# A hybrid attention block on one core: stacks of keys and queries in two buffers by halves, feed-forward buffers of their own, and distances spread over 120 quarters

## The reference

```python
dist = _pairwise_l2(x @ w3d.T + b3d)              # sqrt of the sum of three squares
scores = -dist[:, None, :, :] * scale             # causal, then softmax, then @ V, @ wo
...
r = jax.nn.sigmoid(jnp.einsum('btc,dc->btd', xr, W_r))
k_act = jnp.square(jax.nn.relu(jnp.einsum('btc,dc->btd', xk, W_k)))
out = r * jnp.einsum('btc,dc->btd', k_act, W_v)
...
x = x + attn_a(layernorm(x)); x = x + ffn(layernorm(x))
x = x + attn_b(layernorm(x)); x = x + ffn(layernorm(x))
```

## Time and profile before

| | us |
|---|---|
| median of 3 runs | 2093.7 |
| lowest, highest | 2085.45, 2105.44 |
| the profiled execution's own time | 2109.85 |
| its span | 2108.1 |
| busy in it: PE, DVE, ACT, POOL | 1849.2, 1467.0, 1323.7, 728.2 |

### The profile page before, as it was taken

One profiled execution on the slowest core, in us unless ns is written; L12 is line 12 of the kernel. 1 busy time (PEld: TensorE's weight loads), 2 busy tenths in 40 slices (PEclk: granted clock), 3 DMA queues, 4 the chain that ended last, 5 costly groups with the idle time before them and its releaser, 6 DMA issues. The chain is left out here.

```text
span 2108.1 us, 32379 instructions
## 1 busy us (share of the span) xinstructions
PE 1849.2 (88%) x9842; PEld 922.5 (44%) x9842; DVE 1467.0 (70%) x4288; ACT 1323.7 (63%) x2585; POOL 728.2 (35%) x879
## 2 busy tenths in 40 slices
PE   5677898889997999889998899979998899988986
PEld 4453443335543455434543355434544345322423
DVE  5576778767676677667786667766776677768642
ACT  3564355876569565776758665695657766455664
POOL 1342332234333253333443243333532334312313
PEclk8797899999998999999999899989999999989998
DMA  3006113111131112410132111311124101322000
GB/s 85 1 23 123 26 56 67 31 31 32 55 76 31 31 31 82 80 21 12 41 110 42 31 31 56 76 31 31 34 83 76 22 11 41 99 33 50 13 21 20
DMA packets 64346, 97.26 MB, mean 46 GB/s; under 512 B 15655, under 2 KB 58029, under 8 KB 58030
## 3 DMA queue, kind: packets, MB, share of 16 engines
q1 hardware_dynamic: 64174, 95.20, 20.2%
HBM read 61.09 MB, written 33.55 MB: 45 GB/s over the span
## 5 line engine op out<-in xcount | busy, mean ns | idle before, releaser
L973 ACT ACTIVATE pt<-exp_bank 128x512 f32<-128x512 f32 (+1 forms) x1216 | 698.9, 582 | 526.6 <-PE exp_bank L935 521.0
L989 DVE CUSTOM_DVE_ANT_0 max_bank<-max_bank,mask 128x128 f32<-128x128 f32 (+3 forms) x1024 | 501.8, 500 | 400.9 <-PE max_bank L922 386.4
L922 PE MATMUL max_bank<-ks,qs 96*128 96x512 bf16 (+3 forms) x1536 | 523.5, 346 | 85.9 <-DVE piece_max L992 44.9
L935 PE MATMUL exp_bank<-qs,ks 98*128 98x512 bf16 (+3 forms) x1536 | 515.4, 342 | 40.0 <-ACT pt L973 37.0
L992 DVE TENSOR_REDUCE piece_max<-max_bank 128x1 f32<-128x512 f32 x512 | 344.1, 686 | 94.4 <-PE max_bank L922 90.2
L954 PE MATMUL o_bank<-pt,v 128*17 128x512 f32 (+3 forms) x3072 | 334.1, 508 | 13.7 <-POOL pt L1011 11.0
L922 PEld LDWEIGHTS max_bank<-ks,qs 96*128 96x128 bf16 x1536 | 150.9, 99 | 399.5 <-DVE piece_max L989 140.9
L1011 POOL TENSOR_SCALAR_AFFINE_SELECT pt<-pt 128x512 f32<-128x512 f32 x256 | 171.5, 670 | 412.6 <-ACT pt L973 411.8
L935 PEld LDWEIGHTS exp_bank<-qs,ks 98*128 98x128 bf16 x1536 | 152.4, 100 | 236.0 <-ACT pt L973 118.5
L633 PE MATMUL side<-vp,p 128*128 128x260 f32 x576 | 171.4, 423 | 28.7 <-ACT p L560 21.0
L412 ACT ACTIVATE xh<-xs,shift,rstd 128x256 f32<-128x256 f32 x256 | 149.7, 596 | 47.8 <-POOL shift L401 47.8
(11 more groups left out here) (119 smaller groups left out, 2348.4 us busy)
## 6 DMA issues: line engine op xcount, KB each, us to landing
parts_dram<-parts SPq DMA_DIRECT2D x64, 384.0 KB, 2.6
qs<-parts_dram SPq DMA_DIRECT2D x192, 128.0 KB, 7.2
ks<-parts_dram SPq DMA_DIRECT2D x32, 384.0 KB, 4.7
xs<-in_L_attn_a_x_dram SPq DMA_DIRECT2D x16, 512.0 KB, 4.2
ks<-parts_dram SPq DMA_DIRECT2D x32, 256.0 KB, 5.4
out_dram<-xs SPq DMA_DIRECT2D x16, 512.0 KB, 3.1
ks<-parts_dram SPq DMA_DIRECT2D x32, 128.0 KB, 5.8
qs<-neg_maxT SPq DMA_DIRECT2D x64, 8.0 KB, 1.9
```

The source lines that it names most:

```text
L922: pe.matmul(max_bank[u % MAX_BANKS][:, 0:k1 - k0], qs[r][0:KROWS, j, P * tile:P * (tile + 1)], ks[r][0:KROWS, j, k0:k1], start=True, stop= ...
L935: mm = pe.matmul(exp_bank[k % EXP_BANKS][:, (q1 - q0) * slot:(q1 - q0) * (slot + 1)], ks[r][:, j, P * kt:P * (kt + 1)], qs[r][:, j, q0:q1] ...
L973: act.activation(pt[:, e % 2, j + 1 - heads:j + 1, 0:w], exp_bank[k % EXP_BANKS][:, 0:heads * w].rearrange("p (j n) -> p j n", j=heads), A ...
L989: dve.tensor_tensor_reduce(scores, scores, mask[:, HALF - w:HALF], 1.0, LOWEST, ALU.add, ALU.max, piece_max[:, j, m:m + 1]).then_inc(max_f ...
```

## The change

- STACKS becomes 2. A stack is loaded and waited for by halves of its 1024 columns: the first half as soon as the 8th piece of the group two before has been used, the second after its 12th, each 16 quarters before its first use. Each half takes 9 DMAs of half the bytes.
- The negated maxima go by halves as well: after the 4th and after the 12th piece, each with its own negation, two transposes, one copy and 8 DMAs (before: once a group, 2 DMAs).
- LEAD becomes 12.
- The feed-forward stages get three buffers of their own (shifted); the square of relu is made in place, and the gate is computed in tm. Their waits on the distances, and those of the distances on them, go. act_transposed waits only for the readers of xt in the stage before.
- Distances of batches 2 to 7 take 120 quarters (4 plus two per 128 columns a piece). ATT1 is -110, FFN2 52, FFN4 168 (82 for the last), PROJ3 110.
- The third square is added by POOL, one quarter before the next piece begins; DVE's instruction at line 468 is gone. The guard is a bias (TINY, 1e-18) of the logarithm. DVE makes the third square for batch 0 alone, ACT for batch 1 too. For batch 0 both of ACT's squares stand before the logarithm of the piece before.
- p1 is reused after the 9th piece, X_BUFFERS is 4, and the rows of ones of the (now two) stacks are written by POOL.

```diff
-STACKS = 3
+STACKS = 2
...
-LEAD = NP + 2
+LEAD = NP
...
-X_BUFFERS = 3
+X_BUFFERS = 4
...
-ATT1, FFN2, FFN4, PROJ3 = -44, 50, 82, 114
+ATT1, FFN2, FFN4, PROJ3 = -110, 52, 168, 110
+LAST_FFN4 = 82
...
+STACK_AT = [4 * (LEAD - 2 * NP + 2 * TPH), 4 * (LEAD - NP)]
...
-PIECE_TIME = [2 + (q1 - q0) // P for _, q0, q1 in KEY_PIECES] + [5, 5, 5]
-PIECE_AT = [34 + sum(PIECE_TIME[:p]) for p in range(NP + 4)]
+SHORT = [2 + (q1 - q0) // P for _, q0, q1 in KEY_PIECES] + [5, 5, 5]
+LONG = [4 + 2 * (q1 - q0) // P for _, q0, q1 in KEY_PIECES] + [6, 6, 6]
...
-    rows = [(4 * NP * (g + 1) + 1, ("maxima", g)) for g in range(GROUPS)]
+    rows = [(4 * (NP * g + (NP if h else TPH)) + 1, ("maxima", g, h)) for g in range(GROUPS) for h in range(2)]
...
-            def distance(p):
...
-                dve.scalar_tensor_tensor(out=sq[:, p % 2, 0, 0:w], in0=sq[:, p % 2, 0, 0:w],
-                                         scalar=TINY, in1=sq[:, p % 2, 2, 0:w],
-                                         op0=ALU.max, op1=ALU.add).then_inc(dist2_ready, 1)
...
-                    act.activation(d, d, ACT.Ln).then_inc(log_done, 1)
+                    act.activation(d, d, ACT.Ln, bias=tiny[:, 0:1]).then_inc(log_done, 1)
...
             for p in range(NP + 1):
+                for k in range(2 if n == 0 and p < NP else 0):
+                    yield at(piece_at(n, p) + k)
+                    square(p, k)
...
+                    yield at(piece_at(n, p + 1) - 1)
+                    pool.wait_ge(sum_ready, NP * n + p + 1)
+                    pool.wait_ge(third_ready, NP * n + p + 1)
+                    pool.tensor_tensor(sq[:, p % 2, 0, 0:w], sq[:, p % 2, 0, 0:w],
+                                       sq[:, p % 2, 2, 0:w], ALU.add).then_inc(dist2_ready, 1)
...
                 if f > 0:
-                    act.wait_ge(ka_ready, 2 * f - 1 + j)
+                    act.wait_ge(v_full, 2 * f)
...
             if group >= STACKS:
-                nc.sync.wait_ge(s_full, EXP_PER_GROUP * (group - STACKS + 1))
+                nc.sync.wait_ge(s_full, exp_before(NP * (group - STACKS) + (2 * TPH if half == 0 else NP)))
...
             for c in range(2):
-                nc.sync.dma_start(qs[r][KROWS + c:KROWS + c + 1, :, :], neg_maxT[:, c, :]
-                                  ).then_inc(crow_ready, 16)
+                for j in range(GH):
+                    nc.sync.dma_start(qs[r][KROWS + c:KROWS + c + 1, j, HALF * h:HALF * (h + 1)],
+                                      neg_maxT[TPH * j:TPH * (j + 1), c, :]).then_inc(crow_ready, 16)
```

More of the change, by code:

```diff
@@ L197, in clock, with p1_at @@
     return lambda k: WRITTEN_AT[start + k]
[L199 to L200 removed]
+P1_REUSE = 2 * TPH + 1
+P1_FIRST = sum(q1 - q0 for _, q0, q1 in KEY_PIECES[:TPH])
+P1_COLS = sum(q1 - q0 for _, q0, q1 in KEY_PIECES[:P1_REUSE])
+P1_PIECE = [sum(q1 - q0 for _, q0, q1 in KEY_PIECES[(P1_REUSE if p >= P1_REUSE else 0):p]) for p in range(NP)]
+def p1_at(kt, t):
+    for p, (k, q0, q1) in enumerate(KEY_PIECES):
+        if k == kt and q0 <= P * t < q1:
+            return P1_PIECE[p] + P * t - q0
 def bass_hybrid(nc, x, wq, bq, wk, bk, wv, bv, wo, bo, w3d, b3d, wkqv, bkqv, w_r, w_k, w_v,
@@ L1014, in sp_att3 @@
             t, j = divmod(u, GH)
-            g, early = divmod(t + 9, NP)
-            if j == 0 and early == 0 and STACKS <= g < GROUPS and (g % NG or g == NG):
-                sp_stack(g)
-            n, late = divmod(t - NS, NS)
-            if j == 0 and late == 35 and 0 <= n < B - 2:
+            for half in range(2):
+                g, early = divmod(u - STACK_AT[half], 4 * NP)
+                if early == 0 and STACKS <= g < GROUPS and (g % NG or g == NG):
+                    sp_stack(g, half)
+            n, late = divmod(t - 2 * NS, NS)
+            if j == 0 and late == 13 and 0 <= n < B - 2:
                 for h in range(2):
@@ L1207, in schedule @@
         def schedule(setup, attention, maxima, output, stage):
-            parts = list(setup) + [maxima(g) for g in range(GROUPS) if maxima]
+            parts = list(setup) + [maxima(g, h) for g in range(GROUPS) for h in range(2) if maxima]
             parts += [output(g, h) for g in range(GROUPS) for h in range(2) if output]
```

224 lines of the change are left out of this document (110 added, 114 removed).

## The result

Slower: 2159.9 us (median of 4 runs, 2158.0 to 2166.0) against 2089.8 for the kernel before, measured beside it (2085.5 to 2105.4), a ratio of 1.033 with a 95% interval of 1.027 to 1.039. The forecast was 2041 with a range up to 2100. The profiled execution has a span of 2158.7 us.

What follows compares the result with a forecast made beforehand. ACT was taken to bound the distance stretches and PE the rest. -45 - 6 - 10 - 5 + 13 = -53 us gave a median of 2041 (chance 0.55, own range 2012 to 2070); range for all 1985 to 2100.

Steps and rivals of the forecast that it cites:

- Levelling: Distances of batches 2 to 7: spread out, side jobs fill PE's hollows, PE 94.4% busy throughout; -45 us, bounds 0 and -97.
- Work moved into the ends: First and last turn, PE 88% busy, take att1 of batch 2 and ffn4 of batch 5; -6 us, bounds 0 and -12.
- Set-up and first batches: Start-up: POOL writes the ones instead of DVE, ACT's squares stand ahead; -10 us, bounds +8 and -17.
- LEAD: Tail: two pieces less between the passes shorten PE's wait for the last group's maxima; -5 us, bounds 0 and -8.
- Maxima by halves: Transposes of the maxima: 64 more on PE, with waits for DVE's negation; +13 us, between 0 and +17.6.
- Stacks and SP: Stack halves and maxima's rows on SP: 9 to 11 of 20 us, and 4.6 us for eight issues, hidden; 0.
- Sum on POOL: Third square's sum on POOL, written 3 quarters (3.8 us) ahead of ACT's logarithm; costed at nothing.
- Rival B: ACT's logarithm waits for POOL's sum as for DVE's; -45 and -6 lost, median 2092; chance 0.18.
- Rival C: POOL comes late for the masks that PV needs, PE stops; +84 us, median 2124, slower; chance 0.10.
- The clock: Distance stretches: PE's granted clock of 0.90 rises towards 0.97; at most 17 us, 6 taken within the -45.
- Rival A: Even load keeps the clock up and waits short, so levelling gives its bound -97; median 1990; chance 0.17.

Runs made afterwards that it cites:

- b_table: Changed kernel with the old table of stages and short distance pieces in every batch, still 12 pieces between the passes; 2127 us.
- m: Changed kernel with old table, short distance pieces, 14 pieces between the passes and maxima transposed once a group, POOL's third sum kept; 2098 us.
- i_new_whole: Changed kernel with 14 pieces between the passes and maxima transposed once a group; new table and POOL's third sum kept; 2146 us.
- p: i_new_whole with short distance pieces in every batch, the rest of the new table kept; 3.2 points slower than m.
- h_whole: g_lead14 with the maxima transposed once a group again (64 transposes and 64 DMAs instead of 128 and 512); 2100 us.
- c_both: Changed kernel with 14 pieces between the passes and the old table with short distance pieces; 2140 us, ratio 1.0219.
- g_lead14: Changed kernel with old table, short pieces, 14 pieces between the passes, third sum and batch 1's third squares on DVE; 2138 us, ratio 1.0202.
- e: b_table with the third sum on DVE again, 12 pieces between the passes; 1.7 points slower than b_table.
- d_dve_sum: Changed kernel with the sum of the third square on DVE again, all else as changed; 2137 us.
- j: i_new_whole with the third sum on DVE instead of POOL; 2154 us.
- s_after_148: Changed kernel with the second feed-forward (FFN4) at 148 instead of 168; 1.9 points faster than the changed kernel.
- q_dmas_twice: Changed kernel with the DMAs of the maxima doubled, 16 a half instead of 8, each half the size; 4 points slower than the changed kernel.
- n_whole_16: h_whole with the rows of the maxima written by 16 DMAs a group instead of 2; 244 us slower.

## Why the prediction was wrong

In the order of its steps, with what stood against each:

- **Levelling, -45: the step that failed.** Taken together with the table that it needs, it measured +1.8 points (37 us; b_table to the changed kernel) or +2.3 (48; m to i). Two parts of it were right in kind. ACT's 90% stretches and the wait of 70.3 us went, and longer distance pieces do help, by 19 us with everything else equal (p to i). Wrong was the sentence that then "the whole turn should run as the rest does now", at 94.4% PE: over the 1200 us PE is at 90.1%, and the rest fell from 94.8 to 92.1%. The reserve was read from busy shares; but the stages that were moved brought waits with them, 20.5 us more of idle time in the four middle turns for the same work. Moving FFN4 to 168, which the prediction treated only as filling a hollow, costs 2.7 points alone. And the wait that went was hardly on PE's way: with the kernel before's own distance and table, cutting it from 49.5 to 12.5 us is worth 0.05 points (h to m), nothing within the noise. (The spread itself was smaller than the text says: by PIECE_TIME the short pieces take 60 quarters, not 52.)
- **Work moved into the ends, -6.** Turns 1 and 8 take 17 and 20 us more than before, turns 2 and 7 12 less. Against b_table the ends cost 20 us and give back 13.5: +6, not -6. Ends with idle time do not take work for free when the same engines wait in them.
- **Set-up and first batches, -10.** The first maximum matmul is 2.1 us earlier, not 10. h_whole has the whole start-up except batch 1's squares, and there it is 2.2 us earlier and the kernel is level. So DVE's three writes of the ones stood mostly beside the chain; no run moves them alone.
- **LEAD, -5.** The tail, where the term was taken, did get shorter: what follows the last maximum matmul takes 75.3 us for 77.9 (b for c). Over the whole kernel, by halves, two pieces less are worth -0.7 points (14 us) with POOL's sum and the old table, -3.3 with the new table, +1.0 with DVE's sum. The prediction put the rest of the kernel at nothing, and that is where the difference is made.
- **Maxima by halves, +13: right sign, size wrong by three to four.** 2.1 and 2.3 points (g to h, c to m) at 14 pieces, 4.4 with the new table. Busy 9.0 and PE's wait for the negation 3.2 (13.2 against 10.0), 12 in all, are as forecast. Another 10.7 us are the wait for the half stacks, which the next step held hidden (g and h); the remaining 15 of the 38 between these two traces are spread and stay open.
- **Stacks and SP, 0.** For the stacks themselves this is right (h_whole). For the rows of the maxima it is not. The prediction's 4.6 us for eight issues was right (4.89, and 573 ns each), and against PE's slack it hid them. It left out what stands behind them in SP's order, half stacks and stored parts, and who waits for those: PE 11.3 us in g_lead14 and 10.8 in c_both. In the changed kernel itself PE never waits for a stack; what SP costs there shows only when its DMAs are doubled.
- **Sum on POOL.** Rival B said ACT would wait as before, from POOL: 7.0 us, refuted. Rival C said the masks would be late: PE's wait at o_bank for POOL is 1.7 us where it was 11.0, refuted, though its side, slower, was the right one. The rule that two-input work belongs on VectorE (the Trainium skill, "GPSIMD Engine Reference", section 4.1) gives a sign that came true in one setting only: a sum of 512 columns takes 1273 ns on POOL in the trace after, 1.8 times DVE's 724, and moving all 96 costs nothing at 14 pieces with the old table (h to m), gains 1.7 points at 12 pieces with it (e to b), and costs 1.3 in the change as made (d_dve_sum to the changed kernel). At 14 pieces with the new table the difference, 0.4 points, is within the intervals (i and j).
- **The clock, 6 of the -45.** Rival A's hope for it had its mirror image. Both traces have 0.943, but the one before is not typical of its kernel: beside the first four runs the kernel before had 0.946 to 0.951, and the changed kernel's four executions 0.938 to 0.946. Where the hollow went (s_after_148) the clock is 0.953 to 0.957 in its four executions, with 0.944 to 0.954 for the kernel before beside it.

Put together by the runs: 0 for stacks, buffers and start-up, 0 for the sum on POOL, +2.3 points for the halves at 14 pieces, -0.7 for 12 pieces, +1.8 for the table, are unrounded the 3.3 points of the change. They must come out so, since each step starts where the last one ended, and this is one path only; since the parts do not add (the sum on DVE is worth -1.3, 0 or +1.7 by its surroundings), another order gives other terms. By the other path they are 2.3 for the table and 1.1 for the halves with 12 pieces. By both the table is the largest part. Without halves, at 14 pieces, the change is still slower than the kernel before (i_new_whole, 2.2 points). Why the sum on DVE is 1.3 points faster beside the new table, with 12 pieces, stays open: PE idles 18 us less there (267.5 for 285.7), spread over many waits. So does which wait of the layer norm's chain makes the place 168 bad, as against 148.

## What to carry to other kernels

Where several in-order lists are interleaved by a table, a stretch of an idle engine is not a reserve that another stage can be moved into: move one stage alone and time it before several numbers are changed, because one number can eat what the others bring (here 168 for 148, more than half of the loss). Compare busy shares over the same work, not over the same stretch of time. A wait of an engine other than the bottleneck does not say what its removal is worth: here it was nothing at the old distance and 35 us two pieces nearer. And count small DMAs by what their issue takes on the queue and by what stands behind them there, not by when their bytes land.

## What was not expected of the hardware

- Issuing a DMA takes SP's queue about the same time over a wide range of sizes: 558 ns for 0.5 KB (q_dmas_twice), 573 for 1 KB (the changed kernel), 592 for 8 KB (the kernel before), all medians between on-chip buffers; six of 64 KB from DRAM take 2.77 us, 0.46 each. So splitting a DMA multiplies its cost there: 512 of 1 KB fill 293 us of a queue where 64 of 8 KB filled 38, and the landing times of the page don't show it. The Trainium skill, "Perfetto Trace Analysis", "DMA Instruction — HWDGE (DVE, Sync)", has the sequencer free for its next instruction only when it is through with the descriptors and its own increments. The trace agrees in that each issue holds the queue, by these 573 ns; what fills them it does not show.
- A wait of PE of 5 us costs more than itself. Over the 30 waits of more than 3 us in n_whole_16 between 200 and 2200 us, the granted clock is 0.56 on the mean in the first 5 us behind the wait, 0.95 in the next 5 and 1.00 in the 5 after that. 171 us of such waits made 244 us.
